# The key mask of the first attention stage added on TensorE instead of in VectorE's maximum

## The reference

```python
qp = (q @ Wq.T + bq).reshape(-1, H, seq, HD)
kp = (k @ Wk.T + bk).reshape(-1, H, seq, HD)
vp = (v @ Wv.T + bv).reshape(-1, H, seq, HD)
scores = jnp.einsum('bhqd,bhkd->bhqk', qp, kp)
scores = jnp.where(pad_mask == 0, -jnp.inf, scores)
scores = jnp.where(attn_mask == 0, -jnp.inf, scores)
attn = jax.nn.softmax(scores / sqrt(HD), axis=-1)
out = jnp.einsum('bhqk,bhkd->bhqd', attn, vp).reshape(-1, seq, D)
```

## Time and profile before

| | |
|---|---|
| time, median of 3 runs | 2583.99 us (2581.66 to 2585.85) |
| profiled execution, own time | 2583.99 us |
| its span | 2582.2 us |
| TensorE busy | 96% of the span |
| VectorE busy | 74% |
| ScalarE busy | 52% |
| GpSimd busy | 37% |
| mean granted TensorE clock | 0.984 |

### The profile page before, as it was taken

How to read it: one execution, slowest core, us unless ns; L and a number is a source line. 1 busy time by engine, 2 the same in 40 slices (tenths; PEclk the granted TensorE clock), 3 DMA queues, 4 the chain that set the end, 5 groups by cost and what they waited for, 6 DMA issues and landing times.

```text
span 2582.2 us, 59319 instructions
## 1 busy us (share of the span) xinstructions
PE 2486.7 (96%) x22882; PEld 1879.5 (73%) x22912; DVE 1904.5 (74%) x4731; ACT 1346.0 (52%) x2001; POOL 948.9 (37%) x1158
## 2 busy tenths in 40 slices
PE   6999999999999999999999999899999999999998
PEld 4666666677777778777776666667777678888877
DVE  4788877676666666687779999988888876666662
ACT  0333333454444444455556676666766765555553
POOL 0011111244444443344444667665444432222221
PEclk7999999999999999999999999988999999999999
DMA  2231110122111111132222222212322221111120
GB/s 89 63 103 35 31 36 27 60 73 72 60 60 61 60 52 53 53 99 84 85 94 94 93 88 82 78 66 84 123 92 96 92 77 59 58 58 60 56 92 13
DMA packets 125935, 181.66 MB, mean 70 GB/s; under 512 B 39657, under 2 KB 45977, under 8 KB 125466
## 3 DMA queue, kind: packets, MB, share of 16 engines
q1 hardware_dynamic: 105178, 174.97, 19.5%
q0 software_dynamic: 20480, 2.91, 0.9%
HBM read 40.12 MB, written 4.19 MB: 17 GB/s over the span
## 4 chain that ended last, share of the span: by engine, by line
PE 80%; DVE 13%; ACT 3%; issue 2%; POOL 1%; DMA 0%; SPq 0%; DVEq 0%; ACTq 0%
PE ps_pv L812 11%; PE ps_nat L621 10%; PE ps_st L640 10%; PE ps_misc L908 9%; PE ps_misc L734 6%; PE ps_misc L844 4%; PE ps_misc L771 3%; PE ps_misc L877 3%; DVE mx L1200 3%; PE ps_misc L823 2%; PE ps_misc L878 2%; PE ps_misc L879 2%; DVE ps_nat L1194 2%; PE ps_misc L861 2%; PE ps_st L644 2%
## 5 line engine op out<-in xcount | busy, mean ns | idle before, releaser
L975 ACT ACTIVATE pt<-ps_st 128x1024 f32<-128x1024 f32 (+1 forms) x768 | 759.8, 989 | 742.6 <-PE ps_st L640 365.0
L1200 DVE TENSOR_REDUCE mx<-ps_nat 128x4 f32<-128x1024 f32 x512 | 624.3, 1219 | 271.3 <-PE ps_nat L621 267.5
L1321 POOL DMA_DIRECT2D q_st<-shifts_t x640 | 382.2, 603 | 455.3 <-DVE shifts_t L1215 454.5
L812 PE MATMUL ps_pv<-pt,vaug 128*32 128x256 f32 (+1 forms) x6144 | 381.8, 379 | 2.2 <-ACT pt L975 2.2
L640 PE MATMUL ps_st<-q_st,k_st 64*128 64x256 f32 (+1 forms) x2560 | 323.5, 331 | 23.7 <-ACT pt L975 20.3
L640 PEld LDWEIGHTS ps_st<-q_st,k_st 64*128 64x128 f32 x2560 | 193.0, 186 | 203.6 <-issue 148.2
L1345 POOL TENSOR_TENSOR rstd<-var,half_pow 128x2 f32<-128x2 f32 x144 | 102.2, 710 | 545.4 <-DVE var L1042 544.4
L621 PE MATMUL ps_nat<-k_st,q_st 64*128 64x256 f32 (+1 forms) x2560 | 270.5, 288 | 27.4 <-DVE mx L1200 25.8
L812 PEld LDWEIGHTS ps_pv<-pt,vaug 128*32 128x32 f32 x6144 | 173.6, 110 | 133.8 <-issue 26.4
L1194 DVE CUSTOM_DVE_ANT_0 ps_nat<-ps_nat,on 128x256 f32<-128x256 f32 x512 | 201.0, 455 | 91.4 <-PE ps_nat L621 91.4
L1353 POOL TENSOR_TENSOR xn<-xn,tiles 128x512 f32<-128x512 f32 x128 | 167.4, 1308 | 237.4 <-DVE xn L1046 223.1
(11 more groups left out here) (141 smaller groups left out, 4745.2 us busy)
## 6 DMA issues: line engine op xcount, KB each, us to landing
k_st<-qk SPq DMA_DIRECT2D x480, 128.0 KB, 2.1
q_st<-qk SPq DMA_DIRECT2D x480, 128.0 KB
q_st<-shifts_t POOLq DMA_DIRECT2D x640, 4.0 KB, 1.8
weights<-in_weights SPq DMA_DIRECT2D x19, 512.0 KB, 4.8
cT<-in_ctx_t SPq DMA_DIRECT2D x32, 256.0 KB, 2.8
cn<-in_ctx SPq DMA_DIRECT2D x32, 256.0 KB, 2.9
xT<-in_x_t SPq DMA_DIRECT2D x16, 256.0 KB, 3.4
xn<-in_x SPq DMA_DIRECT2D x16, 256.0 KB, 3.3
```

The source lines that it names most:

```text
L812: last = nc.tensor.matmul(ps_pv[32 * j:32 * j + 32, c, q0:S], vaug[:, rot, kh, s, :], pt[:, at_p, s % 2, kh * S:(kh + 1) * S - q0], start= ...
L975: nc.scalar.activation(pt[:, g % PT_SLOTS, :, 0:used], ps_st[:].rearrange("p j a b -> p j (a b)")[:, :, 0:used], ACT.Exp, scale=SCALE).the ...
L1200: last = nc.vector.reduce_max(out, ps_nat[:], AX)
L1321: nc.gpsimd.dma_start(rows[:, b], shifts_t[32 * b:32 * b + 32, i, :]).then_inc(split_in[rot][i], 16)
```

## The change

In stage 0 the mask of the natural side is added on TensorE, by four products of `ident_b` with `mask0` into `ps_nat`, as it is done in `ps_st`. DVE then takes the maximum with the same TENSOR_REDUCE as the other stages. `nat_done` is now given by the last mask product. In the changed kernel the line numbers are moved by one or more: nat is L620, `nat_mask` L624, st L641, `st_mask` L645, the maximum L1193.

```diff
@@ in nat_part and nat_mask
-                    last = hf == 1 and attention(n) != 2
+                    last = hf == 1 and attention(n) not in (0, 2)
                     return nc.tensor.matmul(ps_nat[:, j, hf, 0:keys], lhs, rhs, start=hf == 0, stop=last)
 
-                def nat_mask(j, hf):
+                def nat_mask(e, j, hf):
+                    if attention(e[1]) == 0:
+                        return nc.tensor.matmul(ps_nat[:, j, hf, :], ident_b[:], mask0[:, hf, :], start=False, stop=hf == 1)
                     return nc.tensor.matmul(ps_nat[:, j, hf, hf * P:(hf + 1) * P], ident_b[:], causal[:],
                                             start=False, stop=hf == 1)
@@ in scores
-                            if nat and not apart and attention(nat[1]) != 2:
+                            if nat and not apart and attention(nat[1]) not in (0, 2):
                                 last_nat.then_inc(nat_done, 1)
...
-                    if nat and attention(nat[1]) == 2:
+                    if nat and attention(nat[1]) in (0, 2):
                         for j in range(2):
                             for hf in range(2):
-                                last_nat = nat_mask(j, hf)
+                                last_nat = nat_mask(nat, j, hf)
                         last_nat.then_inc(nat_done, 1)
@@ on VectorE, kind "nat"
-                        if a == 0:
-                            if n == 0 and i == 0:
-                                dve.wait_ge(const_made, 1)
-                            for j in range(2):
-                                for hf in range(2):
-                                    scores = ps_nat[:, j, hf, :]
-                                    last = nc.vector.tensor_tensor_reduce(scores, scores, mask0[:, hf, :], 1.0, LOWEST, ALU.add, ALU.max,
-                                                                          out[:, j, hf:hf + 1])
-                        elif a == 2:
+                        if a == 2:
                             nc.vector.reduce_max(out[:, :, 0], ps_nat[:, :, 0, 0:P], AX)
                             last = nc.vector.reduce_max(out[:, :, 1], ps_nat[:, :, 1, :], AX)
                         else:
                             last = nc.vector.reduce_max(out, ps_nat[:], AX)
```

More of the change, by code:

```diff
@@ L18 @@
 FLOOR = -1.0e28
-LOWEST = -3.0e38
 EPS = 1e-5
```

## The result

| | before | changed |
|---|---|---|
| median | 2583.85 us (4 runs, 2581.66 to 2585.85) | 2624.2 us (4 runs, 2621.15 to 2629.13) |
| profiled execution, own time | 2583.99 us | 2630.97 us |
| its span | 2582.2 us | 2629.2 us |

The ratio is 1.0158, with a 95% interval of 1.014 to 1.0177: 36 to 46 us slower. A second set of runs of the changed kernel gave 1.0175 (1.0158 to 1.0192). The profiled execution of the changed kernel is not among its four runs and is slower than all of them.

A forecast was written before the change was run, and what follows sets the result against it. TensorE was taken to bound stage 0. New products +57.6, half clock +2.3, pauses given back -5.3, beginning -1.5 and end of stage -1.9 summed to +51.2 us: 2584 + 51 = 2635 us, range 2618 to 2648.

The forecast's parts named there:

- What bounds stage 0: Stage 0: PE bounds it, with 0.46 us of slack in a unit of 26.89; DVE is less than 2% behind.
- The new products: Stage 0 on PE: four added products cost 0.45 us in each of 128 steps, 57.6 us; bounds 0.34 and 0.61.
- The steady unit: Steady part of stage 0: the period of eight steps goes from 26.89 to about 30.0 us (+3.6 - 0.46).
- The pauses of 0.24 and 0.22: PE's two waits for DVE per unit, after L812 and L719; both go, -5.3 us over stage 0.
- The loop over the exponential: Scores, exponential, next scores in stage 0: grows by 0.45, from 2.96 to 3.41 us, as long as PE's own work.
- The loop over the maximum: Scores, maximum on DVE, next scores in stage 0: grows by 0.13, from 2.96 to 3.09 us, and does not bind.
- The clock: Five stage 0 steps at half clock, masks costing twice: +2.3 us; doubt of some 3.5 us from an early stretch.
- rival 4: Stage 0: new products fill the short pause ahead of the first mask, 0.34 per step; +37, 2621 us; chance 0.12.
- VectorE as the bound: Rival 2: DVE's queue sets stage 0's pace, so each step gains 0.35 to 0.37; -47, 2537 us; chance 0.05.
- hidden masks: Rival 3: the masks hide in free time on PE that the weight-load share suggests; no change, 2584 us; chance 0.03.
- the dearer mask: Rival 1: a group of four costs 0.54 instead of 0.45 on PE; +63, 2647 us; or pauses stay, 2644; chance 0.17.

The follow-up runs named there:

- the relief of DVE alone: The changed kernel without the new mask products in the first attention, VectorE taking the plain maximum; 2570.04 us, ratio 0.9961 to the kernel before.
- the mask twice: The changed kernel with the four new mask products put out twice in each step; 2674.36 us, ratio 1.0374 to the kernel before.
- the run with the old reduction: The changed kernel with VectorE's four custom instructions kept, so only the TensorE products are added to the kernel before; 2631.71 us, ratio 1.0202.
- the other order: The changed kernel with the mask into the transposed scores ahead of the mask into the natural ones; 2625.25 us, ratio 1.0177 to the kernel before.

## Why the prediction was right, and its sizes

**What bounds stage 0.** Right. PE paused 0.46 us per unit as read from the distances between starts, the relief of DVE alone took 0.55 off the period, and the added products moved it by 2.94 us. The rule on the share of weight loads, from the Trainium skill, page "Perfetto Trace Analysis", section "Identifying the Most-Contended Engine", would have left a third of PE free. PEld is busy 68.60 us of 100 before. With the mask twice PE is busy 99.69 of 100 us, and PEld only 73.51:

```profile
200.00:300.00 100.00, 99.69 (x1022) 73.51 (x1024) 58.34 (x109) 30.75 (x36) 13.41 (x12) 1.00 0.10 30
```

In this kernel that share never comes near 100 although PE has nothing to wait for.

**The sum by stretches.** The forecast of +51.2 us splits over the time line as follows, from the first profiles and from the second ones (95.11 and 102.76 us are the same step, and so are 417.75 and 461.20):

| stretch | forecast | measured | second profiles |
|---|---|---|---|
| to the first steady unit (95.11) | +8.9 | +7.7 | +6.7 |
| twelve steady units | +37.9 | +35.8 | +35.7 |
| rest of stage 0 | +4.4 | +2.1 | +3.6 |
| stages 1 to 5 | 0 | +1.5 | +5.3 |

The second profiles sum to +51.4, which is the forecast by luck: 5.3 of it is the later part, where the kernels are alike.

**The new products.** 0.45 us was taken, and 0.44 to 0.45 was measured, in full: 57 us. The bounds of 0.34 and 0.61 were both wide of it.

**The steady unit.** Forecast +3.14, measured +2.94. The pauses of 0.24 and 0.22 went as worked out: L813 leads to the next scores after 1.00 and L720 after 0.96. They went by the longer work on PE, as the run with the old reduction shows; the prediction had both reasons in its sum and did not tell them apart. The missing 0.2 are hundredths in many steps: two transposes lead to scores after 0.53 now instead of 0.56 and 0.59, and in most steps both groups of mask products take 0.43 to 0.45 instead of 0.45. I had looked for pauses only where the trace names DVE.

**The loop over the exponential.** This step of the prediction failed; it matters at the beginning of the stage only. I read the 0.21 us from the end of the exponential to the next scores as that loop's own delay, and took it to be 2.96 us long, as long as the loop over the maximum. It was 2.79. In the changed kernel it does bind in a few early steps, and there the delay can be read:

```profile
79.14 1.02 ACT L976 ACTIVATE pt<-ps_st 128x1024 f32<-128x1024 f32 x1 [1.61 <-PE ps_st L645]
...
80.21 0.48 PE L620 MATMUL ps_nat<-qk 17*128 17x256 f32 x2 [0.68 <-ACT pt L976]
```

The exponential ends at 80.16, and the scores start 0.05 later. So those steps grew from 2.96 to 3.24 and not to 3.41. In three early steps that is 0.5 us less. The run with the relief of VectorE alone, with no new products and no wait for DVE, shows such a step at 2.80:

```profile
67.81 0.48 PE L620 MATMUL ps_nat<-qk 17*128 17x256 f32 x2
...
70.61 0.48 PE L620 MATMUL ps_nat<-qk 17*128 17x256 f32 x2 [0.68 <-ACT pt L976]
```

The rest of what the beginning fell short by (1.2 us in the first profiles, 2.2 in the second) is not accounted for; the clock there changes from one profile to the next.

**The loop over the maximum.** Right: at the beginning a step of natural scores alone went from 2.87 us to 2.99, where it was to gain 0.45 and lose 0.3. The two loops with the old reduction (3.50 forecast, 3.51 measured) and with the other order (3.54, 3.53) came out of the same terms. At the end of the stage the way over DVE (441.21 to 448.26 before, 486.81 to 493.64 changed) went from 7.05 us to 6.83, where 6.88 was worked out.

**The clock.** Five steps at half clock were taken as given. The last step of stage 0 ran at half clock before and at full clock after. Its value products show it, L812 before and L813 changed:

```profile
465.83 3.10 PE L812 MATMUL ps_pv<-pt,vaug 128*32 128x256 f32 x32
```
```profile
512.51 1.93 PE L813 MATMUL ps_pv<-pt,vaug 128*32 128x256 f32 x32
```

This step was to grow by 0.9 and became 1.16 shorter. That is 2.1 us, nearly the whole gap of the third stretch (2.3). In the second profile of the kernel before this step ran at the full clock, and the third stretch then grew by 3.6:

```profile
464.72 1.93 PE L812 MATMUL ps_pv<-pt,vaug 128*32 128x256 f32 x32
```

In the first profiles the time came back in the next stage, where another step ran slow, and is most of the +1.5 there. The forecast had named a doubt of 3.5 us for the clock at the beginning; the later part alone differed by 6.3 us between two profiles of one kernel.

**The time.** The profile's +47.0 us lies 4 under the forecast. The medians, +40 in the first set and +43 in the second, lie a few more below it; against the 12 runs of the kernel before (2577.06) the second set of the changed kernel is +49. The stage itself grew by 45.5 and 46.1 us. So the mechanism was right and the size some 5 us too large, by small terms that nearly all err on one side. By the time alone the prediction couldn't be told from rival 4, half hidden masks, whose 2621 is nearer to 2624.2 than 2635 is. What rules that rival out is the time line: it wanted the new products to fill a pause of 0.1 us ahead of the first mask, but the scores lead to the first mask product after 1.08 us as before (226.02 to 227.10, and 233.03 to 234.11), and the new group adds its 0.44 behind them. The doubled mask can't tell the two apart, since a second group would cost its full time under both. The other rivals fell too: VectorE as the bound by the relief alone, which gives 12 to 14 us and not 47; hidden masks by the products alone (+50.7 us in stage 0); the dearer mask by its 0.44.

## What to carry to other kernels

Read an engine's slack from the distances between starts of the same sequence, with and without the wait: a chain of waits names whoever came last, by however little. Here work moved from an engine that waits to one that hardly does cost its full time there, and the relief was worth only the pauses it ended. Before moving a computation, ask whether it is needed where it stands: the mask on the maximum was not, for the inputs used here, and leaving it out gave more than either place for it.

## What the runs showed of the hardware

The bf16 mask products on TensorE cost by their columns: four of 256 or two of 512 take 0.44 us alike at the full clock, with a weight load for each. A TENSOR_REDUCE over 1024 elements in PSUM takes 1.22 us, while four passes that also add the mask, with their accumulator reads, take 1.63. And one and the same kernel, profiled twice, was granted a mean clock of 0.85 and 0.94 in the same stretch of 100 us, and its time after stage 0 differed by 6.3 us.
